# Two cross-attention layers on one core: layer 1's softmax factors turned and spread by VectorE, the last block's residual added by TensorE, low parts and tiles of the tail regrouped, and smaller moves at the start

## The reference

```python
# layer 0: 16 heads of 64, mask over the 128 keys, one global maximum
qh, kh, vh = (q @ Wq + bq), (k @ Wk + bk), (v @ Wv + bv)
attn = einsum(qh, kh) * mask
attn = exp(attn - max(attn)) * mask
attn = attn / (sum(attn, -1) + 1e-15)
x = layernorm(einsum(attn, vh) @ Wo + bo + x) * gamma + beta
# layer 1: 16 heads of 32, plain softmax with scale 1/sqrt(32)
attn = softmax(einsum(x @ Wq.T, ctx @ Wk.T) / sqrt(32))
x = layernorm(einsum(attn, ctx @ Wv.T) @ Wo.T + bo + x) * gamma + beta
```

## Time and profile before

| | |
|---|---|
| median of the runs | 865.46 us |
| the profiled execution's own time | 866.75 us |
| its span, first to last instruction | 865.0 us |
| TensorE busy | 836.3 us (97%) |
| VectorE busy | 590.4 us (68%) |
| ScalarE busy | 426.0 us (49%) |
| GpSimd busy | 451.1 us (52%) |
| granted TensorE clock, mean | 0.995 |

### The profile page before, as it was taken

The page is one execution under the profiler, slowest core; times in us unless marked ns, Lnnn a source line. Parts: engine busy times, 40 slices in busy tenths (PEclk is TensorE's granted clock), DMA queues, the critical chain, the costliest instruction groups (busy, mean ns, idle before and its releaser), DMA issues.

```text
span 865.0 us, 12719 instructions
## 1 busy us (share of the span) xinstructions
PE 836.3 (97%) x4688; PEld 570.1 (66%) x4688; DVE 590.4 (68%) x1272; ACT 426.0 (49%) x570; POOL 451.1 (52%) x277
## 2 busy tenths in 40 slices
PE   8999999999999989899999999999999999999986
PEld 6777475665748464386677677587676776776745
DVE  3568666766767585876776766757657767666697
ACT  4415473645545354634553644534636536444362
POOL 2022403224040422247889679588786896892636
PEclk9999999999999999999999999999999999999999
DMA  9408525161515234986431432513514314311001
GB/s 333 171 34 299 202 100 210 49 234 63 220 63 197 85 126 155 273 307 174 136 109 50 147 98 69 174 50 100 158 61 153 115 50 146 98 50 50 1 25 73
DMA packets 50157, 112.63 MB, mean 130 GB/s; under 512 B 4656, under 2 KB 10544, under 8 KB 50096
## 3 DMA queue, kind: packets, MB, share of 16 engines
q1 hardware_dynamic: 49376, 111.23, 38.2%
q10 hardware_dynamic: 720, 0.60, 0.2%
HBM read 77.74 MB, written 34.08 MB: 129 GB/s over the span
## 4 chain that ended last, share of the span: by engine, by line
PE 81%; DVE 11%; ACT 2%; issue 2%; POOL 2%; DMA 1%; DVEq 0%; SPq 0%; POOLq 0%; ACTq 0%
PE bank L497 17%; PE bank L498 16%; PE bank L499 16%; PE bank L549 7%; PE bank L529 6%; PE bank L536 5%; PE bank L685 3%; DVE scores L1201 2%; DVE den L1340 2%; PE bank L704 2%; DVE r_split L1343 2%; PE bank L485 2%; PE bank L657 1%; DVE scores L1308 1%; PE bank L714 1%
## 5 line engine op out<-in xcount | busy, mean ns | idle before, releaser
L1528 POOL TENSOR_TENSOR x_lo<-x_raw,x_hi 128x2048 fp32r<-128x2048 f32 (+1 forms) x8 | 35.8, 4471 | 199.1 <-ACT x_hi L877 199.1
L497 PE MATMUL bank<-wo_lo,a_hi 128*128 128x512 f32 x320 | 127.5, 399 | 0.0
L498 PE MATMUL bank<-wo_hi,a_lo 128*128 128x512 f32 x320 | 124.9, 390 | 0.0
L499 PE MATMUL bank<-wo_hi,a_hi 128*128 128x512 f32 x320 | 124.9, 390 | 0.0
L1171 DVE CUSTOM_DVE_ANT_0 scores<-bank,mask_f 128x512 f32<-128x512 f32 x128 | 80.8, 687 | 52.4 <-PE bank L529 52.4
L497 PE MATMUL bank<-x_lo,wq_hi 128*128 128x512 f32 x256 | 101.7, 397 | 4.2 <-DVE q_lo L1160 4.2
L988 ACT ACTIVATE scores<-scores,sh 128x512 f32<-128x512 f32 x128 | 80.3, 710 | 49.9 <-DVE sh L1334 49.9
L1564 POOL TENSOR_TENSOR a_lo<-a_raw,a_hi 128x1024 fp32r<-128x1024 f32 x32 | 77.3, 2417 | 51.8 <-ACT a_hi L968 51.8
L499 PE MATMUL bank<-x_hi,wq_hi 128*128 128x512 f32 x256 | 100.3, 392 | 0.0
L498 PE MATMUL bank<-x_hi,wq_lo 128*128 128x512 f32 x256 | 100.2, 391 | 0.0
L889 ACT ACTIVATE q_hi<-bank,bq_sb 128x512 fp32r<-128x512 f32 x64 | 44.1, 690 | 107.9 <-PE bank L499 104.3
(11 more groups left out here) (179 smaller groups left out, 1685.2 us busy)
## 6 DMA issues: line engine op xcount, KB each, us to landing
u_dram<-u_out SPq DMA_DIRECT2D x8, 2048.0 KB, 7.1
a_raw<-u_dram SPq DMA_DIRECT2D x32, 512.0 KB, 3.6
r_bc<-r_dram SPq DMA_DIRECT2D x56, 256.0 KB, 5.0
x_raw<-x_t SPq DMA_DIRECT2D x8, 1024.0 KB, 5.5
xn<-x_n SPq DMA_DIRECT2D x8, 1024.0 KB, 5.2
xb_dram<-xn SPq DMA_DIRECT2D x8, 1024.0 KB, 5.2
z<-xb_dram SPq DMA_DIRECT2D x32, 256.0 KB, 2.8
out<-z SPq DMA_DIRECT2D x6, 1024.0 KB, 7.2
```

The lines of the kernel that those rows point to most:

```text
L497: nc.tensor.matmul(dst, lh, rl, start=first, stop=False)
L498: nc.tensor.matmul(dst, ll, rh, start=False, stop=False)
L499: return nc.tensor.matmul(dst, lh, rh, start=False, stop=last)
```

## The change

1. **Factors of layer 1.** `divisors1`, `r1_high`, `save_u1` and `spread1` on TensorE are gone, with the constants `hs1` and `low_rows` and their loads. `factors1` (VectorE) turns the bank of sums into SBUF by 32x32 blocks, takes maximum and reciprocal of 4 of each 32 columns only (64 elements a partition), and `spread1` (VectorE now) turns each head's column, broadcast 32 times, back into 512 columns. `attention1` multiplies the values straight from their banks. `rows0(i, 2)` now stands behind all of `attention1`.
2. **Order in the loop.** `normal1` of tiles 0 and 1 stands behind `q1_high(i, 2)`, tiles 2 and 3 behind `q1_high(i, 3)`. In block 0 `a0_high(1, 0)` stands behind `yt_high(0, 2)` and `(0, 3)`, and `divisors0(6, 7)` with its reciprocal behind `v1_copy(1)`.
3. **The tail.** TensorE writes the residual of each tile into its bank with the identity (`residual_last`), so that `output_last` accumulates on it; the statistics and the centring read the bank. `attention_last` and the high parts go chunk by chunk in halves. GpSimd makes all low parts. Tiles 2 and 3 of block 6 are scaled, biased and stored one by one.
4. **Last block of layer 0.** `x_and_bias(7)` waits for the masked probabilities of block 6, and its store is issued later. The first four heads of block 7 are exponentiated and masked in two parts.
5. **Start.** The context is loaded in two halves and the first 128 columns of the keys' weights on ScalarE's queue; `bv_sb` is loaded later; the selector isn't loaded. GpSimd waits for `bq1_ready` ahead of the low part of block 2's x.

```diff
@@ tensor: the loop
                 output0(i, 2)
-                if before:
-                    spread1(i - 1, 0)
-                    spread1(i - 1, 1)
-                output0(i, 3, 0, C0 // 2)
-                if before:
-                    spread1(i - 1, 2)
-                    spread1(i - 1, 3)
-                output0(i, 3, C0 // 2)
+                output0(i, 3)
@@ vector
+            def factors1(i):
+                dve.wait_ge(sums1_psum_ready, i + 1)
+                if i > 0:
+                    dve.wait_ge(spread1_ready, C1 * i)
+                nc.vector.transpose(den1[:], SUM1_BANK[:]).then_inc(turned1_ready, 1)
+                dve.wait_ge(turned1_ready, i + 1)
+                nc.vector.tensor_scalar(turned(slice(0, C1)), turned(slice(0, C1)), 1e-36, None,
+                                        ALU.max).then_inc(den1_ready, 1)
+                dve.wait_ge(den1_ready, i + 1)
+                nc.vector.reciprocal(turned(slice(0, C1)), turned(slice(0, C1))).then_inc(rec1_ready, 1)
+            def spread1(i, c, half=None):
...
+                row = turned(c, blocks)
+                nc.vector.transpose(SPREAD[c % 2][:, cols], row.unsqueeze(2).to_broadcast([P, row.shape[1], 32])
+                                    ).then_inc(spread1_ready, 1)
             def attention1(i, c):
...
-                nc.vector.tensor_tensor(a1_raw[:, c, :], a1_raw[:, c, :], TQ_BANKS[c % 2][:],
+                nc.vector.tensor_tensor(a1_raw[:, c, :], L_BANKS[c][:], SPREAD[c % 2][:],
                                         ALU.mult).then_inc(attn1_ready, 1)
@@ vector: the loop
-                    divisors1(i - 1)
+                    factors1(i - 1)
+                    spread1(i - 1, 0)
+                    spread1(i - 1, 1)
                     attention1(i - 1, 0)
+                    spread1(i - 1, 2)
                     attention1(i - 1, 1)
-                rows0(i, 2)
-                if before:
+                    spread1(i - 1, 3)
                     attention1(i - 1, 2)
                     attention1(i - 1, 3)
+                rows0(i, 2)
...
                 if i == 0:
                     v1_copy(0)
-                    divisors0(6, 7)
-                    factors0(slice(0, P), 3, 2, NB)
...
                     v1_copy(1)
+                    divisors0(6, 7)
+                    factors0(slice(0, P), 3, 2, NB)
@@ tensor: the tail
+            def residual_last(n):
...
+                nc.tensor.matmul(LAST_Z[n][:], ident[:], resid_of(i, n // 2)[:, n, :], start=True,
+                                 stop=False).then_inc(resid_psum_ready, 1)
...
+            sums1(i, 0)
+            sums1(i, 1)
+            values1(i, 0)
+            values1(i, 1)
+            residual_last(2)
+            sums1(i, 2)
+            values1(i, 2)
+            sums1(i, 3)
+            values1(i, 3)
+            for n in (0, 1, 3):
+                residual_last(n)
@@ vector: the tail
+            for half in range(2):
+                spread1(i, 0, half)
+                for c in range(C1):
+                    if c + 1 < C1:
+                        spread1(i, c + 1, half)
+                    attention_last(half, c)
+            def statistics_last(n):
+                dve.wait_ge(o1_ready, QT * i + n + 1)
+                nc.vector.bn_stats(st1[:, n, :], LAST_Z[n][:]).then_inc(bn1_ready, 1)
@@ gpsimd
             def x_and_bias(i):
                 pool.wait_ge(xn_loaded, 16 * (i + 1))
+                if i == NB - 1:
+                    pool.wait_ge(probs_ready, HG * (NB - 1))
...
+            scales1(i - 1, 2, 3)
+            scales1(i - 1, 3, 4)
+            out_tile(i - 1, 2, False)
+            out_tile(i - 1, 2, True)
             for half in range(2):
...
+                for c in (0, 2):
+                    pool.wait_ge(a1_hi_ready, C1 * (i + half) + c + 2)
...
+                    nc.gpsimd.tensor_tensor(a1_lo[:, c:c + 2, cols], a1_last[:, c:c + 2, cols], f(a1_hi[:, c:c + 2, cols]),
+                                            ALU.subtract).then_inc(a1_ready, 1)
+                out_tile(i - 1, 3, half == 1)
@@ scalar
-            act.wait_ge(k0_loaded[0], 32)
+            act.wait_ge(ctx_loaded[0], 16)
+            act.wait_ge(ctx_loaded[1], 16)
...
-                exponential(NB - 1, j)
+                if j == 0:
+                    exponential_first(0)
+                    exponential_first(1)
+                else:
+                    exponential(NB - 1, j)
```

More of the change, by code:

```diff
@@ L895, in exponential, with exponential_first @@
                 nc.scalar.activation(four, four, ACT.Exp, bias=neg_mx[:]).then_inc(exp_ready, 1)
+            def exponential_first(part):
+                act.wait_ge(shift_ready, NB)
+                two = scores[:, HC0 * part:HC0 * (part + 1), :]
+                nc.scalar.activation(two, two, ACT.Exp, bias=neg_mx[:]).then_inc(exp_first_ready if part == 0 else exp_ready, 1)
             def wo0_high(half):
@@ L1069, in _ @@
                 q1_high(i, 1)
-                if before and more:
+                if not before:
+                    a0_high(1, 2)
+                q1_high(i, 2)
+                if before:
                     normal1(i - 1, 0)
                     normal1(i - 1, 1)
-                elif more:
-                    a0_high(1, 2)
-                q1_high(i, 2)
-                if i == NB - 1:
-                    normal1(i - 1, 0)
-                    normal1(i - 1, 1)
-                elif before:
+                else:
+                    a0_high(1, 3)
+                q1_high(i, 3)
+                if before and more:
                     normal1(i - 1, 2)
                     normal1(i - 1, 3)
-                elif more:
-                    a0_high(1, 3)
-                q1_high(i, 3)
                 for h in range(H1 // 2):
@@ L1483, in _ @@
[L1483 to L1494 removed]
+            rows1(i - 1, 2)
```

299 lines of the change are left out of this document (135 added, 164 removed).

## The result

The changed kernel took 850.65 us (median of four executions, 850.0 to 851.89), the kernel before 865.45 beside it: a ratio of 0.9828, 95% interval 0.9811 to 0.9845. Forecast were 845.9 and a range of 839 to 853. The profiled execution has a span of 849.2 us (850.99 by its own time) against 865.0: 15.8 us less where 19.6 were forecast.

A forecast was written before the change was run, and what follows sets the result against it. TensorE (busy 836.3 of 865.0 us) bounds the kernel. Blocks 1-7 -10.6, layer 0's end -4.7, first heads -0.6, start -1.05 -0.65, block 0 +1.9, tail -3.9: -19.6 from 865.46 gives 845.9 us, range 839 to 853.

The forecast's parts named there:

- Block 0: Loop's block 0: later divisors delay stores of r; L1450 waits, TensorE loses 0.8, then 1.1 in block 1: +1.9 us.
- block 0's stores are later: Rival: block 0's stores land later than forecast, +4.5 us, 850.4 us in all; chance 0.13.
- the period: Sign: a loop block takes some 57.8 us instead of 59.45; forecast wrong if under 57.3 or over 58.5.
- a stall of over 2 us in a new place: Sign against the forecast: it is wrong if a stall of over 2 us stands in a new place.
- Blocks 1 to 7: Loop: TensorE sheds 2.3 us in each of blocks 1 to 6, 0.75 given back, and 1.0 in block 7: -10.6 us.
- VectorE's chain: VectorE in loop blocks: turn 0.73, reciprocal 0.55, spreads and products 5.4 us; from sums at 610.67 to 617.6, not late.
- growing or port-bound transposes: Two rivals: transposes grow with columns, 887 us, chance 0.03; transposes take the port shared with GpSimd, 857.5 us, chance 0.07.
- Last block of layer 0: End of layer 0: moved bias no longer holds up VectorE's mask; TensorE's wait and lower clock go: -4.7 us.
- First heads: Block 7, layer 0: heads in two parts let TensorE start 1.7 us earlier, but only 0.6 us is gained.
- Start: Program start: shorter wait for first weights, -1.05 us, and VectorE's mask at 72.60 less held up, -0.65 us.
- The second term: Start, at 72.60: the mask waiting for GpSimd's bias comes some 0.7 us earlier without the selector's load: -0.65 us.
- Tail: Program end: halved spreads and products, residual on TensorE, last addition gone; the end moves by 3.9 us.

The follow-up runs named there:

- Experiment 8: Changed kernel with layer 1's low and high parts ahead of layer 0's second tile in GpSimd's and ScalarE's queues, blocks 1 to 6: 846.02 us, ratio 0.9779.
- experiment 9: Changed kernel, but GpSimd's bias addition for block 7's rows no longer waits for block 6's masked probabilities: 856.29 us, ratio 0.9898.
- Experiment 10: Changed kernel, but the first four heads of block 7 in layer 0 are exponentiated and masked whole again: 853.32 us, ratio 0.9851.
- experiment 6: Changed kernel, but SyncE loads block 7's sums only behind the factors of block 1's first two tiles: 851.83 us, ratio 0.9831.
- experiments 1: Changed kernel, but the store of the last block's biased rows (1 MB) is issued in its old place: 851.4 us, ratio 0.9842.
- experiment 2: Changed kernel, but in block 0 ScalarE makes the queries' first two high parts ahead of the second tile's: 851.6 us, ratio 0.9848.
- experiment 4: Changed kernel with the last biased rows' store and the factors of blocks 6 and 7 both in their old places: 847.21 us, ratio 0.9783.
- experiment 11: Changed kernel, but in the tail GpSimd's scaling of block 6's tile 2 waits for VectorE's maximum: 850.93 us, ratio 0.983.

## Why the prediction was right, and where it was off

The largest steps came as forecast, and by the mechanism that was forecast. Block 0 did not. That the total is in the range all the same, 4.75 us above the forecast, is in part luck: the other errors were small or offset each other, and the start's gain came partly from the clock. The rival "block 0's stores are later" gives 850.4 us, nearly the 850.65 measured, but by a mechanism that did not occur. Of the prediction's own signs the period held (57.9 us a block), and "a stall of over 2 us in a new place" came true against it: the 2.7 us at `q_lo`, which no term foresaw.

- **Blocks 1 to 7, the largest step, right.** Predicted 2.3 gone and 0.5 + 0.25 given back; measured 2.36 gone, 0.60 given back at L764 and 0.17 behind it. (For the second, the prediction has `yt_lo` at 633.0; its own numbers, 633.93 less 0.66, give 633.3.) From 416.2 to 734.4 the kernels part by 8.84 us; 6 x 1.6 less the 1.1 of block 1 is 8.5. Block 7: 0.8 for 1.0. Experiment 8 shows cause and size of what is given back: with GpSimd's queue turned it is all regained.
- **VectorE's chain, right.** 512 columns are turned in 0.72 us (0.73), the reciprocal takes 0.55 (0.55), all of it 7.0 (6.9). The rivals on growing or port-bound transposes are refuted: fourteen spreads of 512 columns in each of the two tiles have means of 0.71 and 0.69 us, while GpSimd is busy beside them.
- **Last block of layer 0, right**: 4.9 for 4.7, and experiment 9 turns it back. By the Trainium skill's rule on the shared port pair (SBUF - State Buffer, Who interferes with whom), the traces agree: 6.05 us beside the bias, 2.28 without. First heads: 0.84 for 0.6. Half an exponential and half a mask are 2.1 us by the prediction's own rows, not 1.7; the start moved by 1.85. Experiment 10 gives 1.9; the lower clock in that stretch, 6 us for 3, is the difference that its trace shows.
- **Start, too low**: 2.56 for 1.05 + 0.65. The second term was right (0.67). The first was 1.9. TensorE starts 1.16 earlier (5.17 for 6.33), and then the kernel before starts its key products 0.43 us apart until 9.5 where the changed one starts them 0.22 apart from the first on, which adds 1.5; a wait for weights at 12.9 takes 0.8 back. Half the pace is what matmuls show at the lower clock (L501 to L503 at 402 to 404 us: 0.43 for 0.23), though the view has 1.00 for these windows. The prediction had no term for it, and part of it is chance: the twelve experiments have the changed kernel's start, and at 20 us they lie between 0.34 ahead of it and 1.20 behind. What of it the change brings, one trace of the kernel before can't tell.
- **Block 0, the step that failed.** Predicted: L1450 waits for the stores of r, 0.8, and 1.1 in block 1. Measured: 4.4, and 0.5 (in block 1 TensorE loses 1.05 at L764, in the blocks after it 0.58). The stores went out when I said (394.49, which is 402.95 in the old time; 402.7 forecast), but L1450 (now L1466) did not wait for them: it starts at 398.03, right behind `q_lo`. The loads behind them were late as forecast: GpSimd waits 3.83 us for the third tile's `r_bc`. I asked what the moved *factors* would make late, and not what the 8.3 us that TensorE had gained ahead of this stretch would run into. It ran into 6 MB of transfers, 1 MB of them moved there by the change, that gained only 5.0 us. In the earlier trace rows I read landings as a property of the transfer; 32 KB took 13.5 us in experiment 6, behind the 2 MB of u and what was issued before it. How the 4.4 us divide stays open: the wait of 2.7 and the clock behind it can be taken away (1, 2), but at 416.2 only 0.9 and 2.0 of the 5.1 and 5.4 us that this had given at 404 were left, since two more links (the third tile behind the stores, the collision with `wo_lo`) come next. That experiment 4 was 3.4 us faster in four executions without a trace suggests that the links can be cut together; it isn't shown, and the clock was higher in them too.
- **Tail, term mis-sized**: 2.1 for 3.9. Of the 1.8, 1.0 is the maximum stretched beside GpSimd, shown by experiment 11: I took 0.2 for the maximum without asking what GpSimd does at that moment. Another 0.4 is the first half's spreads and products, 3.17 us (829.46 to 832.63) for 2.8, and 0.3 had gone before: the sums are ready 13.4 us earlier (826.89 for 840.25), where TensorE was 13.7 ahead at 812.
- **Sum.** 19.6 forecast, less 3.6 (block 0) and 1.8 (tail), plus 0.9 (start), 0.2 and 0.24 (end of layer 0), 0.1 in the blocks: 15.6, within 0.2 of the 15.8.

## What to carry to other kernels

When a change makes the bounding engine reach a phase earlier, list the transfers that this phase waits for and ask whether they move up as much. Here a small store behind large transfers landed no earlier for being issued 8.6 us earlier. Move an engine's late queue entries before buying it less work: turning two entries of GpSimd's queue (experiment 8) gave a third of what the whole change gave. A wait removed from a chain of similar links gave little here (experiments 1 and 2); look at the next two links first, and test the edit at its own place in the trace, beside executions of the same code that show what chance does there.

## What the runs showed of the hardware

- VectorE's additions and maximum with a scalar (TENSOR_SCALAR), from SBUF to SBUF, were stretched beside a GpSimd instruction, down to 64 columns: two additions on 64x128 took 0.59 us in six runs, and 1.49, 2.71 and 4.33 in others, the maximum over 64 columns 0.20 or 0.97 to 1.23. Stream transposes (0.71 and 0.69) and reciprocals (0.55 for 64 columns) between the same memories were not.
- The lower clock comes in some executions and not in others after the same stretch of work: behind the products of L695 that start 0.5 to 0.6 us apart, at 816 to 819 us, the granted clock was 0.50 to 0.63 in experiments 1, 4 and 6 and 1.00 in the changed kernel, 1.3 to 1.4 us each time, and TensorE lost nothing there in the other nine. Of four executions of experiment 2 one had a mean of 1.000 and was 3 us faster than the rest.
- The first products of a program ran at half pace for a while, not always as long: 0.43 us apart until 9.5 us in the trace before, 0.22 from the first on in the changed kernel's. At 20 us the thirteen executions of one start (the changed kernel and its experiments) lie up to 1.5 us apart.
- The same code waited 2.7, 3.0, 3.0, 4.6 and 1.9 us for `q_lo` in block 0 (the changed kernel, experiments 8, 9, 11 and 10): a wait that hangs on a landing was no fixed number.
